# A graph network on one core: ScalarE makes and squares the message rows, VectorE sums the squares over the row groups first

## The reference

```python
def _mlp(h, W, b, gamma, beta):
    h = jax.nn.relu(h @ W + b)
    mu = jnp.mean(h, axis=0)
    var = jnp.mean(jnp.square(h - mu), axis=0)
    return gamma * (h - mu) * jax.lax.rsqrt(var + EPS) + beta
...
message = jnp.concatenate([x[row], x[col], edge_feat], axis=1)
message = _mlp(message, W_msg, b_msg, g_msg, beta_msg)
agg = jax.ops.segment_sum(message, col, num_segments=node_feat.shape[0])
return agg + node_feat
```

## Time and profile before

| | |
|---|---|
| time, median of 3 runs | 8700.39 us (8699.28 to 8712.15) |
| span of the profiled execution | 10,523.1 us |
| POOL busy (most of all engines) | 6521.8 us, 62% of the span |
| PE / DVE / ACT busy | 5795.2 / 4507.0 / 3562.3 us |
| gathers | 6468 (1617 in the message pass, 4851 in attention) |
| message pass, first to last `accumulate` | 562 to 2795 us of the span |

### The profile page before, as it was taken

The page is one execution under the profiler, slowest core; times in us unless marked ns, Lnnn a source line. Parts: engine busy times, 40 slices in busy tenths (PEclk is TensorE's granted clock), DMA queues, the critical chain, the costliest instruction groups (busy, mean ns, idle before and its releaser), DMA issues. The chain is left out here.

```text
span 10523.1 us, 129592 instructions
## 1 busy us (share of the span) xinstructions
PE 5795.2 (55%) x27752; PEld 5101.0 (48%) x27752; DVE 4507.0 (43%) x11640; ACT 3562.3 (34%) x7369; POOL 6521.8 (62%) x6545
## 2 busy tenths in 40 slices
PE   4666666676755555545545555555554545545453
PEld 2155555665644444444444544444444444444443
DVE  6644545455533333333343333333334333333335
ACT  3611111111233333333333333333333333333333
POOL 3455666666366666666656666666665666666665
PEclk6555555555556666666666666666666666666666
DMA  4211111111111111111121111111112111111111
GB/s 130 49 32 36 39 38 39 38 39 39 29 35 34 35 34 34 34 35 34 34 34 35 34 34 34 34 34 35 34 32 36 34 35 34 34 35 34 34 34 30
DMA packets 290251, 394.16 MB, mean 37 GB/s; under 512 B 176393, under 2 KB 183961, under 8 KB 287985
## 3 DMA queue, kind: packets, MB, share of 16 engines
q0 software_dynamic: 206976, 330.75, 16.5%
q1 hardware_dynamic: 61176, 46.25, 1.8%
q10 hardware_dynamic: 22024, 16.47, 0.7%
HBM read 367.38 MB, written 25.63 MB: 37 GB/s over the span
## 5 line engine op out<-in xcount | busy, mean ns | idle before, releaser
L637 POOL DMA_INDIRECT store<-table_a,idx x4851 | 4835.4, 997 | 2626.8 <-issue 1595.4
L1262 PE MATMUL ps<-ident,work 128*128 128x128 f32 x4872 | 1179.2, 417 | 2359.3 <-issue 2226.4
L1279 PE MATMUL ps<-store,work 128*128 x9744 | 1788.8, 355 | 1176.6 <-ACT work L1211 841.1
L1279 PEld LDWEIGHTS ps<-store,work 128*128 128x128 f32 x9744 | 1655.2, 263 | 1379.5 <-issue 1377.7
L778 POOL DMA_INDIRECT store<-table_m,idx x1617 | 1597.5, 988 | 1130.6 <-issue 554.9
L1262 PEld LDWEIGHTS ps<-ident,work 128*128 128x128 f32 x4872 | 928.6, 218 | 2456.7 <-issue 2336.8
L1218 ACT ACTIVATE work<-work,small 128x896 f32<-128x896 f32 x696 | 724.5, 1041 | 3314.6 <-issue 2135.0
L1155 DVE SCALAR_TENSOR_TENSOR work<-dstf,store,select 128x224 f32 x696 | 314.2, 451 | 3116.2 <-issue 1668.3
L1144 DVE CUSTOM_DVE_ANT_0 work<-work,ps 128x896 f32<-128x896 f32 x696 | 756.8, 1087 | 1258.7 <-issue 937.7
L1270 PE MATMUL ps<-ident,work 128*128 128x128 f32 x4872 | 1100.6, 398 | 105.7 <-issue 73.9
L870 PE MATMUL ps<-work 128*128 128x96 f32 x3248 | 817.6, 443 | 615.0 <-DVE work L1058 439.8
(11 more groups left out here) (250 smaller groups left out, 4865.7 us busy)
## 6 DMA issues: line engine op xcount, KB each, us to landing
store<-table_a,idx POOLq DMA_INDIRECT x4851
store<-table_m,idx POOLq DMA_INDIRECT x1617
work<-edge_parts ACTq DMA_DIRECT2D x232, 45.5 KB
edge_parts<-store SPq DMA_DIRECT2D x6, 1617.0 KB, 11.7
work<-edge_parts SPq DMA_DIRECT2D x50, 192.0 KB
table_a<-work SPq DMA_DIRECT2D x12, 606.0 KB, 6.5
work<-table_b ACTq DMA_DIRECT2D x232, 12.0 KB
idx<-in_src_dram SPq DMA_DIRECT2D x116, 28.0 KB
```

What stands on the lines that cost most here:

```text
L637: pool.indirect_dma_start(rows[:, k % RING, j, 0:width], None, table, bass.IndirectOffsetOnAxis(ap=idx[:, k // CHUNK, at:at + 1], axis=0)) ...
L1262: last = pe.transpose(ps[:, 4 + j // 4, (j % 4) * P:(j % 4 + 1) * P], prob[:, par, j, :], ident[:])
L1279: last = pe.matmul(ps[:, 6 + par, 0:D + 1], probT[:, par, j, :], rows_of(at("slot", 3))[:, j, 0:D + 1], start=(j == 0), stop=(j == TPG - 1))
```

## The change

Three things change in a step of the message pass, and one behind it.

The message rows: VectorE's instruction that made `rr` from `vsum` (with relu and factor `inside`) is gone. ScalarE makes `rr` as the plain relu of `vsum` (`message`). Rows outside the window are no longer zero in `rr`; the node sums don't see them, since `eq` is zero there.

The squares: ScalarE squares in 7 instructions of 96 columns instead of one of 672, each with its column of `inside` as scale, which leaves the rows outside out of the squares.

The sum: VectorE reduces the 672 squares to 96 over the row groups (`tensor_reduce`), and then adds these 96 to `square_sums`, which has 96 columns now.

Behind the pass, one matmul over `square_sums` stands in place of 7.

```diff
                 def square(k, par):
                     act.wait_ge(s["rr_ready"], k + 1)
+                    act.wait_ge(s["inside_ready"], k + 1)
                     if not (isinstance(k, int) and k == 0):
-                        act.wait_ge(s["squares_added"], k)
-                    nc.scalar.activation(squares, rr[:, par, :, 0:D], ACT.Square).then_inc(s["squares_ready"], 1)
+                        act.wait_ge(s["squares_reduced"], k)
+                    for j in range(TPG):
+                        last = nc.scalar.activation(squares[:, j, :], rr[:, par, j, 0:D], ACT.Square, scale=inside[:, par, j:j + 1])
+                    last.then_inc(s["squares_ready"], 1)
...
+                def message(k, par):
+                    act.wait_ge(s["v_ready"], k + 1)
+                    if not (isinstance(k, int) and k < 2):
+                        act.wait_ge(s["s_ready"], k - 1)
+                    nc.scalar.activation(rr[:, par, :, 0:D], vsum, ACT.Relu).then_inc(s["rr_ready"], 1)
...
                     if live(1):
+                        message(q - 1, (par - 1) % 2)
                         square(q - 1, (par - 1) % 2)
...
-                    dve.tensor_tensor(square_sums, square_sums, squares, ALU.add).then_inc(s["squares_added"], 1)
+                    dve.tensor_reduce(group_squares, squares.rearrange("p j c -> p c j"), AX.X, ALU.add).then_inc(s["squares_reduced"], 1)
+                    dve.wait_ge(s["squares_reduced"], k + 1)
+                    dve.tensor_tensor(square_sums, square_sums, group_squares, ALU.add).then_inc(s["squares_added"], 1)
...
-                    dve.wait_ge(s["v_ready"], k + 1)
-                    dve.wait_ge(s["inside_ready"], k + 1)
-                    if not (isinstance(k, int) and k < 2):
-                        dve.wait_ge(s["squares_ready"], k - 1)
-                    dve.scalar_tensor_tensor(rr[:, par, :, 0:D], vsum, 0.0, inside[:, par].unsqueeze(2).broadcast_to([P, TPG, D]),
-                                             ALU.max, ALU.mult).then_inc(s["rr_ready"], 1)
...
-                for j in range(TPG):
-                    last = pe.matmul(ps[0:D, 4, 0:1], square_sums[:, j, :], ones[:, 0:1], start=(j == 0), stop=(j == TPG - 1))
-                last.then_inc(s_total, 1)
+                pe.matmul(ps[0:D, 4, 0:1], square_sums, ones[:, 0:1], start=True, stop=True).then_inc(s_total, 1)
```

More of the change, by code:

```diff
@@ L672, in gnn_kernel @@
         squares = work[:, 2240:2240 + TPG * D].rearrange("p (j c) -> p j c", j=TPG)
-        square_sums = work[:, 2912:2912 + TPG * D].rearrange("p (j c) -> p j c", j=TPG)
+        square_sums = work[:, 2912:2912 + D]
+        group_squares = work[:, 2912 + D:2912 + 2 * D]
         weights = work[:, 4096:4096 + 2 * D].rearrange("p (s c) -> p s c", s=2)
@@ L706, in gnn_kernel @@
             "eq_ready", "win_ready", "eqt_ready", "u_ready", "ut_ready", "pre_ready", "v_ready",
-            "rr_ready", "s_ready", "inside_ready", "squares_ready", "squares_added")}
+            "rr_ready", "s_ready", "inside_ready", "squares_ready", "squares_reduced", "squares_added")}
         NODE_BANKS = [4, 5, 6, 0, 1, 2, 3]
```

## The result

The changed kernel takes 8608.72 us (median of 4 runs, 8603.82 to 8615.23), the kernel before 8699.83 beside it (4 runs, 8697.13 to 8712.15): a ratio of 0.9894, 95% interval 0.9882 to 0.9906. It is 91 us faster; 78 were forecast.

A forecast was written before the change was run, and what follows sets the result against it. The prediction took GpSimd's nearly unbroken issuing of gathers as the bound. From the timed median, 8700 - 78 us of gather stretch = 8622 us, everything else hidden or 0; own range 8590 to 8640, wider range 8552 to 8712.

The forecast's parts named there:

- The bound: Whole kernel: GpSimd issues gathers nearly without a pause in timed runs; in the pass the step chain is 11% behind.
- The mechanism: Message pass: gathers starting during L1067 or L1029, long with two SBUF inputs, stand until it ends; mean falls 0.996 to 0.95.
- The size: Stretch removed from the pass's gathers: 66 us from the trace, 102 us as upper bound for starts at any moment; 78 taken.
- 1.19 us a gather: Spacing of undisturbed gathers in timed runs, taken 0.06 us below the trace's 1.25 because the summed 9098 exceeded 8700.
- Half for each instruction: Message pass: L1067 and L1029 each cost gathers 0.22 us a step, 0.44 together, 102 us in 232 steps.
- (b): Rival: the reduce or the rest of VectorE's list still holds gathers; only L1067's share, about half, goes: 8661. Chance 0.07.
- The reduce: VectorE's reduce of 672 elements takes 0.85 us and holds no gathers; VectorE gets 0.61 us less a step, 142 in all.
- ScalarE: Seven squares take 0.367 us each, 2.6 in all, the relu 0.764; ScalarE's step grows 2.6 us, hidden.
- Behind the pass: Six small matmuls fewer, once in a run: 3 us if nothing hides them; taken as 0.
- (a): Rival: the steps bind the message pass, not the gathers; at most 23 us gained, 8677 to 8705. Chance 0.18.
- (c): Rival: VectorE's share of the chain binds the pass, so its 0.61 us a step counts in full: 8558. Chance 0.05.
- (d): Rival: ScalarE becomes the bound of the pass through slower squares, 8760 or 8900 us. Chance 0.12.

The follow-up runs named there:

- e6: Changed kernel with six of the seven gathers of each group in the message pass, the seventh row group zeroed once: 8360.9 us, ratio 0.9613.
- e2: Changed kernel plus an unused two-input VectorE sum of 672 columns a step, where L1067 stood: 8640.6 us, ratio 0.9946.
- e3: Changed kernel plus an unused one-input VectorE reduce of 672 columns a step, where L1067 stood: 8669.2 us, ratio 0.9974.
- e4: Changed kernel with only the ScalarE message rows and seven squares; VectorE's two-input add of 672 squares and the seven end matmuls as before: 8687.0 us, ratio 0.9999.
- e5: Changed kernel with only the reduce and add of 96; message rows by VectorE and one ScalarE square of 672 as before: 8607.2 us, ratio 0.9894.
- e1: The kernel before, unchanged, run again for the second profile of it: 8691.8 us against 8693.0, ratio 0.9998.
- e9: e4 with add_squares moved ahead of add_source on VectorE, same instructions: 8627.7 us against 8689.2, ratio 0.9929.
- e10: Changed kernel with the seven squares of a channel stored side by side, so the reduce reads neighbours and ScalarE writes with stride 7: 8605.5 us, ratio 0.9906.
- e7: Changed kernel with all seven ScalarE squares of a step done twice, the first time into a spare buffer: 8607.6 us, ratio 0.9898.
- e8: Changed kernel plus an unused VectorE tensor_scalar (672 columns times 2) a step, where L1067 stood: 8625.9 us, ratio 0.9918.
- e11: e5 with the squares stored side by side as in e10, one ScalarE square of 672 writing with stride 7: 8639.4 us, ratio 0.9947.

## Why the prediction was right, and where it was not

**The bound: right.** In an execution as long as the timed ones GpSimd issues gathers nearly without a pause (the longest in the pass is 18.9 us, behind the first 224); e6 shows that fewer of them bring 248 us.

**The mechanism: right.** A gather that starts inside a long VectorE instruction with two SBUF inputs waits for its end. e2 and e3 are the same place with two inputs and one: 98 gathers held, and none. The mean gather of the pass fell to 0.948 us (about 0.95 forecast), and the attention layers stayed.

**The size: the bounds held, the lower one was the worse guide.** The sum took 78 us between 66 and 102; the time fell by 91 and the gathers by 97.7, so the term was a fifth too small. The stretch before is 102.4 us in an execution like the timed ones, and 4.7 after. The 66 came from the first profile; that its pauses took gathers out of the way is likely, but not shown. The upper bound matches to 0.4 us, but partly by chance: see the halves.

**1.19 us a gather: wrong.** The prediction made 8700 from 9098 by taking 0.06 us off each gather, on the thought that recording lengthens them. The spacing is 1.25 us with and without: 14 gathers in 17.5 us, and a profile whose span equals its time. What was too much in the 9098 was not the gathers but terms from the disturbed execution: 173 us for the pace of the first 224 gathers (the second profile has them in 279 us, and one pause of 19 us behind them), 251 us of stretch in attention (4622.7 - 4851 x 0.945 = 38.5), and 520 us without gathers (in the second profile 107 + 93 + 77 + 74 + 111 = 462, from the starts of the lines). The same sum with the second profile's terms is 8085 + 462 + 19 + 102 + 39 = 8707, against its span of 8705.6. The error cost little in the forecast: of its numbers only the upper bound rests on the 1.19, and with 1.25 it would be 99 us instead of 102.

**Half for each instruction: wrong.** The upper bound priced L1067 and L1029 at 0.22 us a step each, for gathers that start at any moment, and rival (b) gave 8661 if one of them stays. e4 leaves one and gains nothing; e5 leaves one and gains all. Gathers needn't start at any moment of a step. While the steps run at their own pace the estimate is near for both instructions (0.42 us a step in e1, 0.44 estimated) and for e4's one (0.27 against 0.22), but far off for e5's (0.04). Once the steps wait for landings, they begin a fixed time after a gather, and the next one falls just behind the start of whatever follows `add_source`: e4 then loses 0.52 us a step. What stands there decides, with 97 us in the whole pass for the long add (e4), 23 us for 224 elements (e9), and nearly 0 for a reduce. e9 is the plain test: e4's instructions in another order, 59 us less (56 with each against the kernel before of its own comparison).

**The reduce: right to be harmless, its price wrong.** 1.32 us, not 0.85: its line of short and long reduces held neighbours. With neighbours (e10) it is 0.843, as the line said. So VectorE's busy time on the page fell by 4481.1 - 4467.6 = 14 us, not 142. That was hidden, as the text allowed up to 1.7 us for it. But no step of the working said how much more the chain could bear, and e3 shows it to be some 1.7 us a pair: with 0.86 us more of VectorE in a step (e2) the steps still caught up with the gathers late in the pass, with 1.34 (e3) they ended it.

**ScalarE: right, with a size off.** The seven squares take 1.97 us back to back, 0.28 each, against 2.6 forecast; the page's total rose by 3999.8 - 3543.6 = 456 us, 1.97 a step. The earlier trace rows was too dear by a third: they differ by a bias column, among other things, and which of these it is wasn't tested. The figure from the Trainium skill (VectorE: DVE Perf Modes, The TRN2 errata), an estimated 0.27 us, was nearer. The relu is 0.767 as priced. The one wait that the forecast put aside, `square` behind the reduce, is there:

```profile
L951 ACT ACTIVATE work<-work,small 128x96 f32<-128x96 f32 x1624 | 456.7, 361 | 108.9 <-DVE work L1040 108.8
```

At 109 us it costs nothing, as e7 with twice the squares costs nothing.

**Behind the pass: as taken, 0.** The small matmul (0.45 us) stands beside VectorE's reduce of the node sums, as the seven did before (2.37 us in e1):

```profile
2163.16 6.66 DVE L1439 TENSOR_REDUCE small<-XT 96x1 f32<-96x6250 f32 x1 [0.32 <-PEq L715]
2163.17 0.45 PE L1364 MATMUL ps<-ones,work 128*96 128x1 f32 x2 [1.42 <-PEq L715]
```

**The rivals.** (a), steps that bind, is not this kernel's case, though e3 shows it 1.7 us a pair away. (b) fell in its size, by e4 and e5, and its premise, a reduce that holds gathers, by e3. (c) needed VectorE's relief to count in full: it was 14 us in all, and e10, which does give 0.48 us a step, gains nothing. (d), ScalarE as the bound, fell with e7.

## What to carry to other kernels

Where one engine issues transfers back to back, look at the lengths of its instructions, not only at their number: the median tells what one costs, and those above it name the instruction of another engine that held them. What such an instruction costs depends on where it stands when the issuing engine's next one starts; in a loop that waits for landings this is the same place every time, so that here a long two-input instruction right behind the landing wait was the dearest, and moving it brought two thirds of what removing both did (61.5 us of 91.1). Before a price is read off a single profile, compare its span with the timed runs: one of 10,523 us for a kernel of 8700 says what a gather costs, and little about where the others go.

## What the runs showed of the hardware that was not expected

- By a two-input instruction a gather is held only if it starts after it; started 0.04 us before it, it takes 0.94 us and VectorE its usual 0.86 (e5). A `tensor_scalar` of 672 elements also held gathers that had begun 0.33 to 0.47 us before it (to 1.10 us), and was itself held, to 0.75 us, where it began 0.5 to 0.7 us into one (e8).
- Beside the long two-input instructions, a `tensor_scalar` of 672 elements (0.51 us) holds the gathers that start in it too, 15.2 us in the pass (e8), and so does a two-input one of 224 (0.45 us), up to 23.4 us (e9). No reduce in these runs did, up to 1.34 us.
- A reduce of 7 x 96 elements takes 1.32 us where the seven lie 96 columns apart, and 0.84 where they are neighbours (e10).
- ScalarE pays for a strided output: 96 elements at every seventh place take 0.455 us against 0.361, and 672 take 1.435 (e11) against 0.764.
